# Four conditional layers on one core: the reaction term in a PSUM bank, the identity added behind the transposition, beta on GpSimd, a new order of the slots

## Chip, cores, metric

One Trainium2 chip, one core. The metric is device time in microseconds (us). An item is one of the 128 entries of the batch, a slot is one turn of the loops that take one item further on each engine. A transfer's landing time runs from its issue to the arrival of its completion.

## What is computed

x is 128 items of 128x512 (rows s by columns d), fp32. The reference, cut to what matters:

```python
def cond_residual(x, kind, lang, zX, zY, zR, cat, ...):
    a = tanh(x @ W1 + b1) @ v                       # one score per row
    p = softmax(where(mask[kind], a, -1e30))        # 128x128 per item
    x = x + (p @ x) / count(mask)                   # layer 0
    h = relu(x @ W1l[lang] + b1l[lang])
    y = x + h @ W2l[lang] + b2[lang]
    x = x + layernorm(y) * gamma[lang] + beta[lang] # layer 1
    lap_x, lap_y = second differences, reflected at the ends
    x = x + zX*lap_x + zY*lap_y + zR*x*(1-x)        # layer 2
    return x + x @ W3[cat] + b3[cat]                # layer 3, W3: 64 of 512x512
```

## The kernel before, in words

All five queues are written out by hand in raw form with semaphores: each engine has its own function `slot(s)`, which `run_slots` repeats, and every item is at a different stage on each engine (the number after `s -` says which item a call takes). Nothing else sets the order.

**Stages of an item.** PE projects the item's transpose (`attn_project`, `adapter_project`), ACT takes the tanh, PE spreads the scores and adds the mask (`attn_scores`), DVE finds the row maximum, ACT takes the exponentials, DVE makes the scale and writes scaled probabilities plus the identity (`mix_rows`, L713), PE transposes that (`mix_transpose`) and ACT moves the result (`move_mixT`). With the identity in it one matmul (`pool`, L402) gives x + pooled. DVE reads that bank twice: plus b2 (`add_b2`) and plus beta (`add_beta`, L777). PE adds the adapter (`adapter_up`, L411), DVE and ACT take mean and variance, GpSimd (POOL) the inverse root (`inverse_std`, L865), and `normalize` (L746) writes x2, the input of layer 2.

**Layer 2.** SP issues six DMAs per item (`shift_rows`, L281) that copy x2 from SBUF to SBUF one row up (`below`) and one row down (`above`); POOL adds the two (`sum_rows`, L885) and the left and right neighbours (`sum_columns`, L873). ACT writes c0 - zR*x2 into the SBUF buffer `react` (`reaction`, L539), POOL multiplies it by x2 (`react_times_x2`, L879), DVE adds the columns (`add_columns`, L754) and the rows (`add_rows`, L764) and so has x3.

**Layer 3.** PE transposes x3 (L419), ACT moves it, and `category` (L429) takes four 128x512 matmuls with the 1 MB matrix of the category into one of two banks `ps_out`. POOL adds x3 to the bias b3 (`add_b3`, L892), DVE adds bank and bias (`result`, L739), and SP stores.

**Loads.** Items are sorted by category, and a category's matrix is loaded once (`load_w3`, L259, skipped unless `fresh`) into one of two 1 MB halves. 55 of the 128 items bring a new matrix. In the sorted order (1 is a new one) they are
10011000110011100100001100011010 10001111110010100100001000010000 11000101000101001101110001010100 11010010110011011010001100101000.
b3 is read for every item and spread over 128 partitions (`load_b3`, L267, 256 KB written). SP's slot is: six shifts of item s, w3 of s, store of s-2, b3 of s; its registers for category, fresh and half are read (`load_params`) ahead of the wait for x2. xT and x are loaded from ACT's queue.

**Where items stand before.** x2 of item i is written at the end of DVE's slot i+1, x3 of i in slot i+3, the first category matmul of i is in PE's slot i+4 right behind the scores, and `result` of i in DVE's slot i+4. PE's slot begins with `pool`.

## Time and profile before

| | us |
|---|---|
| median of 3 runs | 1095.55 (1087.53 to 1095.93) |
| profiled execution | 1097.21 |
| its span, first to last instruction | 1095.4 |
| PE busy | 1055.9 (96%) |
| DVE busy | 956.5 (87%) |
| POOL busy | 710.9 (65%) |
| ACT busy | 504.8 (46%) |
| mean granted TensorE clock | 0.998 of full |

The profiled execution stands 1.8 us above its own span and 1.7 us above the median of the runs. Matmul ends are modelled and overlap the next start, so PE's real time for a piece is read from starts, or from the chain, which counts each stretch once. A DMA instruction's length is that of its issue, not of its transfer.

### The profile page before, as it was taken

What the parts mean: (1) busy time and instruction counts of PE and PEld (TensorE: products, weight loads), DVE (VectorE), ACT (ScalarE), POOL (GpSimd) and SP (SyncE); (2) the same over time, 40 slices, a digit from 0 to 9 for tenths busy, and PEclk for the clock granted to TensorE, in tenths of its full rate; (3) what the DMA queues carried; (4) which work ended last, traced back from release to release, by engine and by line L of the source; (5) the groups of instructions that cost most, each with busy time, mean ns of one, the idle gap of its engine ahead of it and who ended that gap; (6) DMA issues with size and microseconds to landing.
All of it is one profiled execution on the core that took longest, in us unless ns stands there. A gap on an engine that the chain in (4) does not pass through costs nothing.

```text
span 1095.4 us, 23744 instructions
## 1 busy us (share of the span) xinstructions
PE 1055.9 (96%) x4912; PEld 656.8 (60%) x4912; DVE 956.5 (87%) x1962; ACT 504.8 (46%) x1422; POOL 710.9 (65%) x665
## 2 busy tenths in 40 slices
PE   6799999999999999999999999999999999999996
PEld 3565666656655656666665566665666565566562
DVE  5799989989989899999888888989898898999994
ACT  3444444444444444445444444444444444444441
POOL 3467667666666676667657666767665766667765
PEclk9999999999999999999999999999999999999999
DMA  8688798678779977876786868887879788897873
GB/s 346 199 260 236 247 293 244 203 250 254 245 230 288 298 239 237 246 229 203 228 266 193 265 198 255 269 266 235 269 241 262 228 268 237 288 276 226 244 241 115
DMA packets 134732, 268.92 MB, mean 246 GB/s; under 512 B 29139, under 2 KB 29157, under 8 KB 127173
## 3 DMA queue, kind: packets, MB, share of 16 engines
q1 hardware_dynamic: 97476, 199.83, 58.7%
q10 hardware_dynamic: 37120, 67.58, 20.4%
q8 instruction: 49, 0.80, 0.3%
q14 instruction: 87, 0.70, 0.2%
HBM read 243.21 MB, written 33.55 MB: 253 GB/s over the span
## 4 chain that ended last, share of the span: by engine, by line
PE 54%; issue 21%; POOL 17%; DVE 6%; DVEq 1%; ACTq 0%; ACT 0%; DMA 0%; POOLq 0%; SPq 0%
PE ps_out L429 23%; POOL b_wide L892 6%; PE ps_adapt L411 6%; PE bank_hidden L383 6%; PE ps_attn L361 6%; PE ps_pool L402 6%; POOL neighbours L873 4%; POOL react L879 3%; PE ps_x3T L419 3%; POOL rstd L865 2%; DVE x L764 2%; PE bank_scores L372 2%; PE bank_hidden L395 1%; DVE res L739 1%; POOL above L885 1%
## 5 line engine op out<-in xcount | busy, mean ns | idle before, releaser
L429 PE MATMUL ps_out<-w3s,x3T 128*128 x1024 | 490.1, 601 | 2.3 <-ACT x3T L496 2.3
L885 POOL TENSOR_TENSOR above<-above,below 128x512 f32<-128x512 f32 x128 | 166.7, 1303 | 226.7 <-DMA above<-x 223.7
L429 PEld LDWEIGHTS ps_out<-w3s,x3T 128*128 128x128 f32 x1024 | 185.1, 191 | 190.6 <-issue 188.7
L764 DVE SCALAR_TENSOR_TENSOR x<-above,wide_rows,react 128x512 f32<-128x512 f32 x128 | 189.5, 1481 | 13.9 <-POOL above L885 12.5
L879 POOL TENSOR_TENSOR react<-react,x 128x512 f32<-128x512 f32 x128 | 175.5, 1371 | 2.4 <-ACT react L539 2.4
L892 POOL TENSOR_TENSOR b_wide<-b_wide,x 128x512 f32<-128x512 f32 x128 | 173.1, 1352 | 1.7 <-DMA b_wide<-in_b 1.7
L865 POOL TENSOR_TENSOR rstd<-var_eps,minus_half 128x1 f32<-128x1 f32 x128 | 70.2, 549 | 132.0 <-DVE var_eps L731 131.9
L517 ACT ACTIVATE square_junk<-ps_adapt,neg_mean 128x512 f32<-128x512 f32 x128 | 88.1, 688 | 139.1 <-DVE neg_mean L692 139.1
L411 PE MATMUL ps_adapt<-w_all,hid 128*128 x256 | 133.0, 601 | 12.6 <-DVE x L746 12.2
L383 PEld LDWEIGHTS bank_hidden<-w_all,xts 128*128 128x128 f32 x1024 | 124.4, 192 | 28.4 <-issue 26.4
L383 PE MATMUL bank_hidden<-w_all,xts 128*128 x1024 | 137.2, 277 | 0.0
L873 POOL TENSOR_TENSOR neighbours<-x 128x510 f32<-128x510 f32 x128 | 133.4, 1042 | 3.6 <-DVE x L746 3.6
L361 PE MATMUL ps_attn<-xts,w_attn 128*128 128x128 f32 x1024 | 135.3, 275 | 0.3 <-issue 0.3
L402 PE MATMUL ps_pool<-xs,mixT 128*128 128x512 f32 x256 | 131.0, 594 | 0.0
L361 PEld LDWEIGHTS ps_attn<-xts,w_attn 128*128 128x128 f32 x1024 | 124.6, 192 | 0.5 <-issue 0.5
L739 DVE TENSOR_TENSOR res<-ps_out,b_wide 128x512 f32<-128x512 f32 x128 | 87.2, 682 | 36.1 <-POOL b_wide L892 26.0
L713 DVE SCALAR_TENSOR_TENSOR mix<-probs,scale,ident 128x128 f32<-128x128 f32 x128 | 108.7, 849 | 0.3 <-issue 0.3
L686 DVE SCALAR_TENSOR_TENSOR ps_adapt<-ps_adapt,x_b 128x512 f32<-128x512 f32 x128 | 89.4, 698 | 17.0 <-PE ps_adapt L411 16.1
L539 ACT ACTIVATE react<-x,c_t,nzr_t 128x512 f32<-128x512 f32 x128 | 102.8, 803 | 2.8 <-DVE x L746 2.8
L502 ACT ACTIVATE probs<-bank_scores,neg_max 128x128 f32<-128x128 f32 x128 | 47.1, 368 | 118.3 <-DVE neg_max L679 118.0
L754 DVE SCALAR_TENSOR_TENSOR react<-neighbours,wide_rows,react 128x512 f32<-128x512 f32 x128 | 96.8, 756 | 0.5 <-POOL react L879 0.5
L722 DVE SCALAR_TENSOR_TENSOR ps_adapt<-ps_adapt,neg_mean,gamma_wide 128x512 f32<-128x512 f32 x128 | 95.5, 746 | 0.1
(111 smaller groups left out, 1281.3 us busy)
## 6 DMA issues: line engine op xcount, KB each, us to landing
w3s<-in_w SPq DMA_DIRECT2D x128, 1024.0 KB
xts<-in_xT ACTq DMA_DIRECT2D x128, 256.0 KB, 4.7
xs<-in_x ACTq DMA_DIRECT2D x128, 256.0 KB, 5.0
b_wide<-in_b SPq DMA_DIRECT2D x128, 256.0 KB, 4.2
out_x<-res SPq DMA_DIRECT2D x128, 256.0 KB, 3.4
below<-x SPq DMA_DIRECT2D x128, 252.0 KB
above<-x SPq DMA_DIRECT2D x128, 252.0 KB
below<-x SPq DMA_DIRECT2D x256, 2.0 KB
```

The source lines that it names most:

```text
L361: mm = pe.matmul(ps_attn, w1_attn[:, k * A:(k + 1) * A], xts[:, r, k, :], start=(k == 0), stop=(k == K - 1))
L383: mm = pe.matmul(ps_xw, xts[:, s.ring(2), k, :], w1_all[:, bass.ds(lang * (K * A) + k * A, A)], start=(k == 0), stop=(k == K - 1))
L402: pe.matmul(ps_pool[:, :], mixT[:, d.ring(2), :], xs[:, d.ring(2), :], start=True, stop=True).then_inc(pool_mm, 1)
L411: pe.matmul(ps_adapt[:, :], hid[:, g.ring(2), :], w2_all[:, bass.ds(lang * D, D)], start=True, stop=True).then_inc(adapt_mm, 1)
L429: mm = pe.matmul(ps_out[j.ring(2)][:, :], x3T[:, j.ring(2), k * P:(k + 1) * P], w3s[:, bass.ds(wslot * (K * D) + k * D, D)], start=(k == 0 ...
L539: nc.scalar.activation(react[:, h.ring(2), :], x2[:, h.ring(2), :], ACT.Identity, bias=c0_t[:, bass.ds(h.n, 1)], scale=nzr_t[:, bass.ds(h. ...
L713: nc.vector.scalar_tensor_tensor(mix[:, p, :], probs[:, p, :], scale[:, p:p + 1], ident[:, :], ALU.mult, ALU.add).then_inc(mix_ready, 1)
L764: nc.vector.scalar_tensor_tensor(x3[:, q, :], above[:, q, :], zy_t[:, bass.ds(i.n, 1)], react[:, q, :], ALU.mult, ALU.add).then_inc(x3_rea ...
L873: nc.gpsimd.tensor_tensor(neighbours[:, q, 1:D - 1], x2[:, q, 0:D - 2], x2[:, q, 2:D], ALU.add).then_inc(neighbours_ready, 1)
L879: nc.gpsimd.tensor_tensor(react[:, q, :], react[:, q, :], x2[:, q, :], ALU.mult).then_inc(react_x2_ready, 1)
L885: nc.gpsimd.tensor_tensor(above[:, q, :], above[:, q, :], below[:, q, :], ALU.add).then_inc(rows_ready, 1)
L892: nc.gpsimd.tensor_tensor(b3_wide[:, q, :], b3_wide[:, q, :], x3[:, q, :], ALU.add).then_inc(x3_b3_ready, 1)
```

## The change

- `react` becomes a single PSUM bank `ps_react`; the two banks `ps_out` become one. The product with x2 moves from POOL to DVE.
- ACT scales the probabilities (`scale_rows`), PE transposes them, and DVE adds the identity as it moves them out of PSUM (`add_identity`). `mix_rows` and `move_mixT` go.
- beta is no longer added by DVE from the bank: POOL adds a table of beta - b2 to `x1_b2` (`add_beta`); the table comes from one more small load and one subtraction at the start. `normalize` waits for it, and the bank of `pool` is free after `add_b2`.
- Every engine's slot is written in a new order. PE's begins with `attn_project`, does the last category matmul of item s-5, and the first three of item s-4 near its end. SP issues the shifts of s, then reads its registers, then w3 and b3 of item s-1, then the store of s-3. POOL's is beta and root of s, `add_b3` of s-2, columns and rows of s-1.

Core of the diff (the context rows of the slots are kept, their removed rows stand in the kernel above):

```diff
@@
...
-        ps_out = [pb("ps_out0"), pb("ps_out1")]
+        ps_react = pb("ps_react")
+        ps_out = pb("ps_out")
...
-        ps_wide = ps_out[0]
-        b2_banks = [ps_out[1], bank_scores]
+        ps_wide = ps_out
+        b2_banks = [ps_react, bank_scores]
...
@@
             def slot(s):
                 if s.inside(B):
-                    cat, fresh, wslot = load_params(sp, CAT, 3, s)
                     shift_rows(s)
-                    load_w3(s, cat, fresh, wslot)
-                if (s - 2).inside(B):
-                    item_m2, = load_params(sp, ITEM, 1, s - 2)
-                    store(s - 2, item_m2)
-                if s.inside(B):
-                    load_b3(s, cat)
-            run_slots(slot, 0, B + 1)
+                if (s - 1).inside(B):
+                    cat, fresh, wslot = load_params(sp, CAT, 3, s - 1)
+                    load_w3(s - 1, cat, fresh, wslot)
+                    load_b3(s - 1, cat)
+                if (s - 3).inside(B):
+                    item_m3, = load_params(sp, ITEM, 1, s - 3)
+                    store(s - 3, item_m3)
+            run_slots(slot, 0, B + 4)
             for r in range(2):
                 sp.wait_ge(res_out[r], 16 * (B // 2))
                 sp.wait_ge(w3_in[r], 16 * (B // 2))
@@
...
-            pe.wait_ge(pick_made, 1)
-            pe.wait_ge(row_rest, 2)
-            spread_b2(0)
-            spread_b2(1)
             def sort_param(what):
...
@@
-            spread_b2(2)
-            spread_b2(3)
+            pe.wait_ge(pick_made, 1)
+            pe.wait_ge(row_rest, 3)
+            for i in range(4):
+                spread_b2(i)
...
@@
-                    if j.is_at_least(2):
-                        pe.wait_ge(res_ready, j.upto(2))
+                    if j.is_at_least(1):
+                        pe.wait_ge(res_ready, j.upto(1))
...
-                    mm = pe.matmul(ps_out[j.ring(2)][:, :], x3T[:, j.ring(2), k * P:(k + 1) * P],
+                    mm = pe.matmul(ps_out[:, :], x3T[:, j.ring(2), k * P:(k + 1) * P],
...
             def slot(s):
...
+                if s.inside(B):
+                    attn_project(s)
+                if (s - 5).inside(B):
+                    wslot, = load_params(pe, WSLOT, 1, s - 5)
+                    category(s - 5, wslot, range(3, K))
+                if (s - 1).inside(B):
+                    adapter_hidden(s - 1)
+                    pool(s - 1)
                 if s.inside(B):
                     kind, = load_params(pe, KIND, 1, s)
...
+                    attn_scores(s, kind)
+                if (s - 4).inside(B):
+                    x3_transpose(s - 4)
                 if s.inside(B):
...
+                    lang, = load_params(pe, LANG, 1, s)
+                    adapter_project(s, lang)
+                if (s - 1).inside(B):
+                    lang_m1, = load_params(pe, LANG, 1, s - 1)
+                    adapter_up(s - 1, lang_m1)
+                if (s - 4).inside(B):
+                    wslot_next, = load_params(pe, WSLOT, 1, s - 4)
+                    category(s - 4, wslot_next, range(0, 3))
                 if s.inside(B):
                     mix_transpose(s)
...
+            run_slots(slot, 0, B + 4)
         @block.scalar
@@
...
+            act.dma_start(base_rows[:, :], lbase).then_inc(lrows_in, 16)
...
-            act.wait_ge(lrows_in, 16)
+            act.wait_ge(row_rest, 1)
...
-            act.wait_ge(row_rest, 1)
+            act.wait_ge(row_rest, 2)
...
@@
-            def move_mixT(b):
-                act.wait_ge(mixT_mm, b.upto())
+            def scale_rows(b):
+                p = b.ring(2)
+                act.wait_ge(scale_ready, b.upto())
+                act.wait_ge(probs_ready, b.upto())
...
-                    act.wait_ge(pool_mm, b.upto(2))
-                nc.scalar.activation(mixT[:, b.ring(2), :], ps_mixT, ACT.Copy).then_inc(mixT_ready, 1)
+                    act.wait_ge(mixT_mm, b.upto(2))
+                nc.scalar.activation(mix[:, p, :], probs[:, p, :], ACT.Copy, scale=scale[:, p:p + 1]
+                                     ).then_inc(mix_ready, 1)
...
             def relu(f, lang):
...
@@
-                if h.is_at_least(2):
-                    act.wait_ge(x3_ready, h.upto(2))
-                nc.scalar.activation(react[:, h.ring(2), :], x2[:, h.ring(2), :], ACT.Identity,
+                if h.is_at_least(1):
+                    act.wait_ge(x3_ready, h.upto(1))
+                nc.scalar.activation(ps_react[:, :], x2[:, h.ring(2), :], ACT.Identity,
...
@@
                 act.dma_start(xs[:, r], x[bass.ds(item, 1)].rearrange("o s d -> s (o d)")).then_inc(x_in[r], 16)
             def slot(s):
...
                 if s.inside(B):
                     item, = load_params(act, ITEM, 1, s)
+                    load_xT(s, item)
+                if s.is_first:
                     load_x(s, item)
...
                     for i in range(4, L):
                         move_b2(i)
+                if (s - 1).inside(B):
+                    attn_tanh(s - 1)
+                if (s - 2).inside(B):
+                    lang_m2, = load_params(act, LANG, 1, s - 2)
+                    relu(s - 2, lang_m2)
+                if (s - 4).inside(B):
+                    reaction(s - 4)
+                if (s - 5).inside(B):
+                    move_x3T(s - 5)
+                if (s - 1).inside(B):
+                    exponentials(s - 1)
+                    move_xw(s - 1)
+                if s.inside(B) and not s.is_first:
+                    load_x(s, item)
+                if (s - 4).inside(B):
+                    column_ends(s - 4)
+                if (s - 1).inside(B):
+                    scale_rows(s - 1)
                 if (s - 2).inside(B):
                     variance(s - 2)
...
+            run_slots(slot, 0, B + 4)
         @block.vector
@@
...
-            def mix_rows(b):
-                p = b.ring(2)
-                dve.wait_ge(scale_ready, b.upto())
+            def add_identity(b):
+                dve.wait_ge(mixT_mm, b.upto())
...
-                    dve.wait_ge(mixT_mm, b.upto(2))
-                nc.vector.scalar_tensor_tensor(mix[:, p, :], probs[:, p, :], scale[:, p:p + 1], ident[:, :],
-                                               ALU.mult, ALU.add).then_inc(mix_ready, 1)
+                    dve.wait_ge(pool_mm, b.upto(2))
+                nc.vector.tensor_tensor(mixT[:, b.ring(2), :], ps_mixT, ident[:, :], ALU.add).then_inc(mixT_ready, 1)
...
             def center(h, lang):
...
@@
-                nc.vector.tensor_tensor(res[:, o.ring(2), :], ps_out[o.ring(2)][:, :], b3_wide[:, o.ring(2), :], ALU.add
+                nc.vector.tensor_tensor(res[:, o.ring(2), :], ps_out[:, :], b3_wide[:, o.ring(2), :], ALU.add
...
             def normalize(h):
...
+                dve.wait_ge(x1_beta_ready, h.upto())
...
+            def react_times_x2(i):
+                q = i.ring(2)
+                dve.wait_ge(react_ready, i.upto())
+                nc.vector.tensor_tensor(ps_react[:, :], ps_react[:, :], x2[:, q, :], ALU.mult).then_inc(react_x2_ready, 1)
...
             def add_columns(i):
...
-                nc.vector.scalar_tensor_tensor(react[:, q, :], neighbours[:, q, :], zx_t[:, bass.ds(i.n, 1)],
-                                               react[:, q, :], ALU.mult, ALU.add).then_inc(columns_ready, 1)
+                nc.vector.scalar_tensor_tensor(ps_react[:, :], neighbours[:, q, :], zx_t[:, bass.ds(i.n, 1)],
+                                               ps_react[:, :], ALU.mult, ALU.add).then_inc(columns_ready, 1)
...
             def add_rows(i):
...
             def slot(s):
-                h = s - 1
-                if h.inside(B):
-                    lang, = load_params(dve, LANG, 1, h)
+                if (s - 1).inside(B):
+                    lang, = load_params(dve, LANG, 1, s - 1)
...
-                if h.inside(B):
-                    add_b2(h, lang)
-                    add_beta(h, lang)
                 if s.inside(B):
                     denominator(s)
...
+                    row_scale(s)
+                if (s - 1).inside(B):
+                    add_adapted(s - 1)
+                    mean(s - 1)
+                if (s - 3).inside(B):
+                    add_columns(s - 3)
                 if s.inside(B):
...
+                    add_identity(s)
                 if (s - 3).inside(B):
                     add_rows(s - 3)
+                if (s - 1).inside(B):
+                    add_epsilon(s - 1)
+                    center(s - 1, lang)
                 if (s - 4).inside(B):
                     result(s - 4)
...
+                if (s - 1).inside(B):
+                    normalize(s - 1)
+            run_slots(slot, 0, B + 4)
         @block.gpsimd
@@
...
+            pool.wait_ge(lrows_in, 2 * 16)
+            nc.gpsimd.tensor_tensor(lang_rows[:, :], lang_rows[:, :], base_rows[:, :], ALU.subtract).then_inc(row_rest, 1)
...
@@
+            def add_beta(h, lang):
+                q = h.ring(2)
+                pool.wait_ge(x1_b2_ready, h.upto())
+                if h.is_first:
+                    pool.wait_ge(beta_moved, L)
+                if h.is_at_least(2):
+                    pool.wait_ge(x2_ready, h.upto(2))
+                nc.gpsimd.tensor_tensor(x1_beta[:, q, :], x1_b2[:, q, :], beta_less_b2[:, bass.ds(lang * D, D)], ALU.add
+                                        ).then_inc(x1_beta_ready, 1)
             def inverse_std(h):
...
@@
                                         ).then_inc(x3_b3_ready, 1)
             def slot(s):
+                if s.inside(B):
+                    lang, = load_params(pool, LANG, 1, s)
+                    add_beta(s, lang)
+                    inverse_std(s)
                 if (s - 2).inside(B):
-                    sum_rows(s - 2)
+                    add_b3(s - 2)
                 if (s - 1).inside(B):
                     sum_columns(s - 1)
-                if (s - 3).inside(B):
-                    add_b3(s - 3)
-                if (s - 1).inside(B):
-                    react_times_x2(s - 1)
-                if s.inside(B):
-                    inverse_std(s)
-            run_slots(slot, 0, B + 2)
+                    sum_rows(s - 1)
+            run_slots(slot, 0, B + 4)
```

SP's queue from its first shifts on (`below`, `above` are the shifts, `w3s` the matrix, `b_wide` the b3 buffer), before:

```order
L281 DMA below<-x 126x512
L281 DMA above<-x 126x512
L281 DMA below<-x 1x16x32 x2
L281 DMA above<-x 1x16x32 x2
L259 ISA
L259 REGISTER_ALU
L259 DMA w3s<-in_w 128x2048
L267 ISA
L267 DMA b_wide<-in_b 128x512
L235 TENSOR_LOAD all_params
L281 DMA below<-x 126x512
```

After, behind the four rows of item 0's shifts, which read like the first four here (these are item 1's):

```order
L284 DMA below<-x 126x512
L284 DMA above<-x 126x512
L284 DMA below<-x 1x16x32 x2
L284 DMA above<-x 1x16x32 x2
L236 TENSOR_LOAD all_params
L260 ISA
L260 REGISTER_ALU
L260 DMA w3s<-in_w 128x2048
L268 ISA
L268 DMA b_wide<-in_b 128x512
```

The loads of item 0 have moved behind the shifts of item 1, and the register reads between those shifts and the loads. POOL's queue, one slot in the steady part, with what each instruction waits for, before:

```order
L885 TENSOR_TENSOR above<-above,below 128x512 [waits shift_in1]
L873 TENSOR_TENSOR neighbours<-x 128x510 [waits columns_ready,x2_ready]
L892 TENSOR_TENSOR b_wide<-b_wide,x 128x512 [waits b3_in0,x3_ready]
L879 TENSOR_TENSOR react<-react,x 128x512 [waits react_ready]
L865 TENSOR_TENSOR rstd<-var_eps,minus_half 128x1 [waits x2_ready,vareps_ready]
```

And after:

```order
L236 TENSOR_LOAD all_params
L860 ISA [waits x2_ready,x1_b2_ready]
L860 TENSOR_TENSOR x_beta<-x_b,beta_less_b 128x512
L868 TENSOR_TENSOR rstd<-var_eps,minus_half 128x1 [waits x2_ready,vareps_ready]
L889 TENSOR_TENSOR b_wide<-b_wide,x 128x512 [waits b3_in0,x3_ready]
L876 TENSOR_TENSOR neighbours<-x 128x510 [waits columns_ready,x2_ready]
L882 TENSOR_TENSOR above<-above,below 128x512 [waits shift_in1]
```

The addition of b3 (`b_wide`) now stands ahead of both neighbour sums and of the next slot's beta and root, where it stood behind the sums.

## Rows read from the trace of the kernel before

**Rows 1.** Chain that ended last, PE's slot around 500 us: start, us, what.

```profile
499.54 0.86 PE ps_pool L402 x2
...
502.45 2.58 PE ps_out L429 x6
505.02 0.11 PE bank_scores L389
...
506.03 0.89 PE ps_attn L361 x8
...
507.58 0.86 PE ps_pool L402 x2
```

**Rows 2.** Waits: who waited for whom, us in total, times, longest.

```profile
POOL above L885 <- DMA above<-x: 223.7, 113, 5.2
...
PE ps_adapt L411 <- DVE x L746: 12.2, 17, 1.3
...
PE bank_scores L389 <- DVE mix L713: 7.9, 4, 2.2
```

**Rows 3.** The page, costliest groups: busy us, mean ns, idle before.

```profile
L764 DVE SCALAR_TENSOR_TENSOR x<-above,wide_rows,react 128x512 f32<-128x512 f32 x128 | 189.5, 1481 | 13.9 <-POOL above L885 12.5
...
L865 POOL TENSOR_TENSOR rstd<-var_eps,minus_half 128x1 f32<-128x1 f32 x128 | 70.2, 549 | 132.0 <-DVE var_eps L731 131.9
...
L713 DVE SCALAR_TENSOR_TENSOR mix<-probs,scale,ident 128x128 f32<-128x128 f32 x128 | 108.7, 849 | 0.3 <-issue 0.3
```

**Rows 4.** Timeline of DVE around 500 us: start, us, instruction.

```profile
499.70 0.74 DVE L746 SCALAR_TENSOR_TENSOR x<-ps_adapt,rstd,x_beta 128x512 f32<-128x512 f32 x1
...
504.43 0.74 DVE L764 SCALAR_TENSOR_TENSOR x<-above,wide_rows,react 128x512 f32<-128x512 f32 x1
505.09 0.68 DVE L739 TENSOR_TENSOR res<-ps_out,b_wide 128x512 f32<-128x512 f32 x1
```

**Rows 5.** Timeline of SP's queue, the slot behind that x2 (items 57 and 58).

```profile
500.50 0.89 SPq L281 DMA_DIRECT2D below<-x  x1
...
503.68 1.74 SPq L281 DMA_DIRECT2D above<-x  x2
505.82 0.10 SPq L259 DMA_DIRECT2D w3s<-in_w  x1
506.60 0.37 SPq L272 DMA_DIRECT2D out_x<-res  x1
507.16 0.34 SPq L267 DMA_DIRECT2D b_wide<-in_b  x1
508.54 0.88 SPq L281 DMA_DIRECT2D below<-x  x1
...
511.53 1.22 SPq L281 DMA_DIRECT2D above<-x  x2
```

**Rows 6.** Timeline of POOL, 508 to 512 us.

```profile
508.14 1.27 POOL L885 TENSOR_TENSOR above<-above,below 128x512 f32<-128x512 f32 x1 [1.68 <-DMA above<-x]
509.37 1.04 POOL L873 TENSOR_TENSOR neighbours<-x 128x510 f32<-128x510 f32 x1
510.36 1.27 POOL L892 TENSOR_TENSOR b_wide<-b_wide,x 128x512 f32<-128x512 f32 x1
```

**Rows 7.** Line L267, all 128 b3 loads.

```profile
DMA to landing us min/median/max: 3.2/4.2/9.9
```

**Rows 8.** DMA issues from 445 to 470 us, no new matrix: count, KB, median landing.

```profile
b_wide<-in_b SPq DMA_DIRECT2D x3, 256.0 KB, 3.7
```

**Rows 9.** The same from 330 to 372 us, every matrix new.

```profile
b_wide<-in_b SPq DMA_DIRECT2D x5, 256.0 KB, 6.4
```

**Rows 10.** Timeline of DVE: first and last of 128 x2, and the last x3.

```profile
32.36 0.75 DVE L746 SCALAR_TENSOR_TENSOR x<-ps_adapt,rstd,x_beta 128x512 f32<-128x512 f32 x1
...
1074.01 0.75 DVE L746 SCALAR_TENSOR_TENSOR x<-ps_adapt,rstd,x_beta 128x512 f32<-128x512 f32 x1
...
1083.40 1.68 DVE L764 SCALAR_TENSOR_TENSOR x<-above,wide_rows,react 128x512 f32<-128x512 f32 x1 [2.72 <-POOL above L885]
```

109 lines of the change are left out of this document (21 added, 88 removed).

## The prediction

> **What bounds the kernel now.** I read the chain that ended last first, because PE is 96% busy. Its slot there has no hole: from one start of the pooling matmul to the next is 507.58 - 499.54 = 8.04 us [rows 1]. 127 such steps are 1021 us. From the end of the first x2 (33.1) to that of the last (1074.8) are 1041.7 us [rows 10], so PE loses 20.6 us in the steady part. The waits name them: 12.2 us for x2 ahead of the adapter matmul and 7.9 us for the mix ahead of its transposition [rows 2], together 20.1. The reader should see that PE bounds the kernel, that DVE is late now and then, and that no more than 21 us can be won in the loop. The matmuls are the same after the change.
>
> Next, why DVE is late. `add_rows` takes 1.48 us on average and the mix 0.85 [rows 3], but `add_rows` has a slot where it takes 0.74 [rows 4]. Both read two SBUF operands. The Trainium skill (SBUF — State Buffer, "SBUF: two separate sides") says that such a DVE instruction and a GpSimd one that reads SBUF shut each other out for the whole instruction. The averages here, twice the undisturbed length, agree.
>
> Last, the transfers, in SP's timeline and the landing times. Before, w3 and b3 of item i are issued right behind x2 of i and used three slots later, so their landing costs nothing. POOL does wait 223.7 us for the shifts [rows 2], without harm.
>
> **The change part by part.**
>
> *DVE's and POOL's work.* DVE loses the beta addition and the two instructions with two SBUF operands; it gains the product in PSUM (bounded by the PSUM and SBUF addition of 0.68 [rows 4] and the 0.74 of a three-operand one) and the identity, 128 wide (0.2 to 0.4; the 0.85 average holds the shut-outs). That is even in plain work and frees (1.48 - 0.74) x 128 = 95 us at `add_rows`, more at the mix. This is worth at most the 20.6 us above, and nothing if something else sets the slot. POOL swaps a product for a beta addition of the same form, 1.27 us. ACT swaps a 128-wide copy for a 128-wide scaling: nothing. The single `ps_out` is read by `result` while PE does some 3.5 us of other pieces, so I cost it at nothing; if that cover went, it would cost what `result` is late, 0.7 us a slot.
>
> *SP's queue.* Here is a wait the old order did not have. Loads of item i-1 are issued behind the shifts of item i, hence behind x2 of i. POOL's `add_b3` of i-1, which needs that b3, stands ahead of both sums of item i and ahead of beta and root of item i+2. DVE's `normalize` of i+2 stands behind `add_rows` of i. So x2 of i leads to b3 of i-1, to POOL's row, to x2 of i+2: a loop over two slots, whose length does not depend on where PE stands. Its parts:
>
> - x2 to the first shift 0.06 (500.44 to 500.50). Issuing the shifts 4.9 us (500.50 to 505.42) or 4.2 (508.54 to 512.75) [rows 5]; I take 4.5.
> - Reading three registers, now behind the shifts: between b3's issue ending (507.50) and the next shift (508.54) lie 1.04 us, part of it perhaps x2 [rows 5]; I take 0.95. Address of w3 0.4 (505.42 to 505.82), its issue 0.1, b3's 0.2. b3 is issued 6.2 us after x2.
> - Landing of b3. Over all slots 3.2 to 9.9 [rows 7]. Issue by issue, the 73 behind a repeated matrix have a median of 3.6, the 55 behind a new one 5.8, as the stretch without new matrices (3.7) and the one with only new ones (6.4) show [rows 8, 9]. The 1 MB goes ahead of it in the same queue.
> - POOL: `add_b3`, columns, rows. From the row sum's start to the next but one are 510.36 - 508.14 = 2.2 us, and the b3 addition takes 1.3 [rows 6]: 3.5.
> - DVE from there: `add_rows` 0.66 (504.43 to 505.09), epsilon 0.1, `center` as long, `result` 0.68, `normalize` 0.74 [rows 4]: 2.8. On POOL meanwhile a register read, beta 1.27 and the root 0.55 [rows 3], then `normalize`: 2.9 at most. I take 2.9.
>
> Sum with a repeated matrix: 6.2 + 3.6 + 3.5 + 2.9 = 16.2 us for two slots, against 2 x 8.04 = 16.08 of PE. It just binds. With a new matrix the 1 MB is issued 6.0 after x2 and b3 0.3 later. Before, b3 went 1.34 behind w3 and landed 5.8 later, with a 256 KB store between them; now there is no store between, so w3's issue to b3's landing is 7.1 less the store's part, which I put at 0.9: 6.2 to 6.4. That makes 12.3 + 6.4 = 18.7; I take 18.8.
>
> Both ends: 15.7 (shifts 4.2, landing 3.4) to 17.0 with a repeated matrix (POOL's path late, landing 4.2), and 17.4 (shifts 4.2, a landing near the shortest of the new ones) to 20 (landing like that of the stretch of new matrices, 6.4, and more).
>
> *The sum.* Let T(i) be the end of x2 of item i. T(i+2) is the later of T(i) + 16.2 (18.8 where the matrix of i-1 is new) and T(i+1) + 8.04. Walked along the order of new matrices given above, with T(0) = 0 and T(1) = 8.04: T(2) = 16.2, T(3) = 26.8 (item 0 is new), T(4) = 34.9, T(5) = 43.0, T(6) = 53.7, and so on to T(127) = 1129.7 (8.90 a slot). An average of the two lengths would give 8.66; the excess is that a late item drags its neighbour's chain with it.
>
> *Start and end.* Before, the first x2 is done at 33.1 and the last instruction ends 20.6 after the last x2. The start gains a subtraction on POOL (about 1.2 us as a row-wide one, beside the sorting) and moves the b2 rows behind the sorting: +1.0, between 0 and 3. At the end x3 of the last item came 10.3 us behind its x2 (1085.1 - 1074.8) [rows 10]; now it comes 6.2 + 3.6 + 3.5 + 0.8 = 14.1 behind: +3.8.
>
> Total against the profiled execution: 1.8 outside the span + 33.1 + 1.0 + 1129.7 + 20.6 + 3.8 = 1190 us. The profiled execution (1097.2) stands 1.7 above the median of the runs; I leave that in the rounding: 1188.
>
> The 1 MB itself has less time too. It is issued 6.0 after x2 of i and PE's first category matmul of i-1 comes some 10 after it when PE runs without holes. If it lands late, PE's three matmuls 2.58 and the transposition 0.11 [rows 1] follow, then `attn_project` 0.89 and the last 0.86 beside DVE's rows, and `result` and `normalize`, 1.4: with a landing of 5.7 that is 6.0 + 5.7 + 2.7 + 1.9 + 1.4 = 17.7, shorter than the 18.8 by b3, so it is not added.
>
> [...]
>
> **Rivals.**
>
> *PE stays without holes (faster).* DVE's shut-outs go, the 20.6 us come back and the loads land in time. For it: 16.2 is near 16.08, DVE's 95 us are real. Against: 55 slots with 1 MB ahead of b3. It decides where b3 behind a new matrix lands within 3.6 us of issue; the shortest of 55 is 3.8. Time: 1097.2 - 20.6 + 4.8 = 1081. The skill's rule on two SBUF operands gives this by itself.
>
> *The loop binds only a little (no change).* New matrices cost 16.5 for two slots: the same walk gives T(127) = 1037, 1098 in all. It needs landings some 2 us shorter than the trace's.
>
> *The 1 MB binds and not b3 (slower, less).* If b3 overtakes the matrix, new slots cost 17.4 and others 16.08: T(127) = 1072.6, 1133 us.
>
> *Transfers in a crowd (slower, more).* In the stretch of new matrices b3 takes 6.4 at the median [rows 9] with three slots of room; with less room xT, too, may be late. 17.0 and 20: T(127) = 1193, 1254 us.
>
> **Chances.** Forecast 0.58, PE without holes 0.06, no change 0.06, the 1 MB binds 0.17, crowd 0.13. The predicted time is the forecast's, 1188. The range leaves out the first two and the far end of the crowd: 1122 to 1248. About 1% is what a measurement tells here: faster 0.06, same 0.05, slower 0.89.
>
> **What would show it.** Right: POOL waits for b3 ahead of `add_b3` in most slots, 1 us or more in the mean and longest behind new matrices; PE's holes stand ahead of the adapter matmul (for x2), its busy share falls to some 89%; x2 of i to x2 of i+2 is near 16.2 or 18.8; `add_rows` takes 0.74 everywhere. Wrong: POOL's `add_b3` never waits for a DMA (then the loop does not exist), or PE's holes stand ahead of the category matmuls, released by the w3 DMA (then the 1 MB binds), or holes in front of `attn_project` released by xT.

## The result, and the profile after

| | before | after |
|---|---|---|
| median of the runs, us | 1095.74 (4 runs) | 1218.46 (4 runs, 1217.53 to 1223.32) |
| ratio | 1 | 1.1137, 95% interval 1.1063 to 1.1211 |
| profiled execution, its span | 1097.21, 1095.4 | 1223.32, 1221.5 |
| mean granted TensorE clock | 0.998 | 0.973 |

The change costs 11%. The page of the kernel after: busy times, granted clock, the chain that ended last by engine and by line, and four of the costliest groups.

```profile
PE 1099.6 (90%) x4912; PEld 663.6 (54%) x4912; DVE 818.8 (67%) x1962; ACT 518.1 (42%) x1422; POOL 681.1 (56%) x666
...
PEclk8899999999999999999999999999999999999998
...
PE 36%; SPq 21%; DMA 18%; POOL 12%; issue 7%; DVE 3%; DVEq 1%; ACT 1%; POOLq 0%; ACTq 0%
PE ps_out L428 16%; DMA b_wide<-in_b 15%; SPq L284 15%; SPq L236 4%; PE ps_adapt L410 4%; PE ps_attn L361 4%; PE bank_hidden L383 4%; POOL above L882 4%; PE ps_pool L401 3%; POOL x_beta L860 3%; POOL neighbours L876 3%; POOL b_wide L889 2%; DVE x L738 2%; SPq L260 2%; DMA w3s<-in_w 2%
...
L428 PE MATMUL ps_out<-w3s,x3T 128*128 x1024 | 508.0, 621 | 79.3 <-issue 63.9
L889 POOL TENSOR_TENSOR b_wide<-b_wide,x 128x512 f32<-128x512 f32 x128 | 162.4, 1269 | 466.9 <-DMA b_wide<-in_b 466.0
...
L751 DVE SCALAR_TENSOR_TENSOR ps_react<-neighbours,wide_rows,ps_react 128x512 f32<-128x512 f32 x128 | 96.7, 755 | 282.3 <-POOL neighbours L876 280.7
...
L761 DVE SCALAR_TENSOR_TENSOR x<-above,wide_rows,ps_react 128x512 f32<-128x512 f32 x128 | 95.3, 745 | 25.7 <-issue 22.1
```

The chain of before was PE's from slot to slot [rows 1]. Now only 36% of it is PE's; SP's queue (the shifts L284, the register reads L236), the landing of b3 and POOL's row hold half of it: the loop that the prediction describes. POOL waits 466 us for b3 ahead of `add_b3`, and DVE waits 281 us for the column sum that stands behind it. `add_rows` takes 745 ns instead of 1481 [rows 3], so DVE is freed, by 137.7 us of busy time, and none of it reaches the end.

DVE's timeline, the counterpart of [rows 10]: the first and the last x2, and the last x3.

```profile
44.01 0.75 DVE L738 SCALAR_TENSOR_TENSOR x<-ps_adapt,rstd,x_beta 128x512 f32<-128x512 f32 x1
...
1195.10 0.74 DVE L738 SCALAR_TENSOR_TENSOR x<-ps_adapt,rstd,x_beta 128x512 f32<-128x512 f32 x1
1209.23 0.75 DVE L761 SCALAR_TENSOR_TENSOR x<-above,wide_rows,ps_react 128x512 f32<-128x512 f32 x1 [0.47 <-POOL above L882]
```

From the first x2 (44.76) to the last (1195.84) are 1151.1 us, 9.06 a slot instead of 8.20. Before they were 1041.7; the first x2 comes 11.7 later, and from the last x2 to the end are 5.0 more.

Two turns of the loop. With a repeated matrix, from the timelines of SP, POOL and DVE, beginning at x2 of item 74 (ended 709.71):

```profile
709.74 0.88 SPq L284 DMA_DIRECT2D below<-x  x1
...
712.74 1.22 SPq L284 DMA_DIRECT2D above<-x  x2
715.50 0.11 SPq L260 DMA_DIRECT2D w3s<-in_w  x1
715.82 0.36 SPq L268 DMA_DIRECT2D b_wide<-in_b  x1
...
719.35 1.27 POOL L889 TENSOR_TENSOR b_wide<-b_wide,x 128x512 f32<-128x512 f32 x1 [3.11 <-DMA b_wide<-in_b]
...
721.57 1.27 POOL L882 TENSOR_TENSOR above<-above,below 128x512 f32<-128x512 f32 x1
722.93 0.75 DVE L761 SCALAR_TENSOR_TENSOR x<-above,wide_rows,ps_react 128x512 f32<-128x512 f32 x1
...
724.96 0.74 DVE L738 SCALAR_TENSOR_TENSOR x<-ps_adapt,rstd,x_beta 128x512 f32<-128x512 f32 x1
```

x2 of item 76 ends at 725.70, 15.99 behind: PE's own two slots. With a new matrix, here as the chain that ended last gives it (start, us, what), from x2 of item 78 (ended 745.46):

```profile
744.80 0.67 DVE x L738
...
745.48 0.88 SPq L284
...
749.76 1.16 SPq L236
...
751.31 0.36 SPq L260
...
751.89 6.07 DMA b_wide<-in_b
...
758.10 0.39 POOL b_wide L889
...
759.31 1.04 POOL neighbours L876
760.35 1.23 POOL above L882
761.58 1.23 POOL x_beta L860
...
763.73 0.67 DVE x L738
```

The register reads take 1.16 us behind the shifts, b3 lands 6.07 after its issue behind the 1 MB, and x2 of item 80 ends at 764.39, 18.93 behind. PE in the same stretch:

```profile
753.86 1.02 PE L410 MATMUL ps_adapt<-w_all,hid 128*128 x2
756.47 2.84 PE L428 MATMUL ps_out<-w3s,x3T 128*128 x6 [1.58 <-issue]
```

PE's largest hole stands ahead of the category matmuls and not of the adapter's. The page calls most of such idle time "issue". Sorted by item, the holes in front of the first category matmul sum to 76.2 us in 42 of the 55 items with a new matrix, and to 3.0 us in the 73 others; so nearly all of it is waits for w3. Two transfers are late, and the experiments had to tell them apart.

Medians below are over items 4 to 123, read from the timelines: two slots (x2 of n to x2 of n+2), apart by whether the matrix of n-1 is repeated or new. In the kernel after they are 16.6 and 19.3 us. Which items are new is read from the length of SP's w3 issue, 0.36 us for a load and 0.11 for a skipped one.

### The profile page after: what moved, and what is told of

It reads as the page before. It is cut to its first block, busy times and chain, and to the rows that moved or that the text cites. A ratio compares the mean times of both kernels' runs of the same rounds, so it can differ in the third digit from the quotient of the medians.

```text
span 1221.5 us, 24130 instructions
## 1 busy us (share of the span) xinstructions
PE 1099.6 (90%) x4912; PEld 663.6 (54%) x4912; DVE 818.8 (67%) x1962; ACT 518.1 (42%) x1422; POOL 681.1 (56%) x666
## 4 chain that ended last, share of the span: by engine, by line
PE 36%; SPq 21%; DMA 18%; POOL 12%; issue 7%; DVE 3%; DVEq 1%; ACT 1%; POOLq 0%; ACTq 0%
PE ps_out L428 16%; DMA b_wide<-in_b 15%; SPq L284 15%; SPq L236 4%; PE ps_adapt L410 4%; PE ps_attn L361 4%; PE bank_hidden L383 4%; POOL above L882 4%; PE ps_pool L401 3%; POOL x_beta L860 3%; POOL neighbours L876 3%; POOL b_wide L889 2%; DVE x L738 2%; SPq L260 2%; DMA w3s<-in_w 2%
## 5 line engine op out<-in xcount | busy, mean ns | idle before, releaser
L428 PE MATMUL ps_out<-w3s,x3T 128*128 x1024 | 508.0, 621 | 79.3 <-issue 63.9
L889 POOL TENSOR_TENSOR b_wide<-b_wide,x 128x512 f32<-128x512 f32 x128 | 162.4, 1269 | 466.9 <-DMA b_wide<-in_b 466.0
L751 DVE SCALAR_TENSOR_TENSOR ps_react<-neighbours,wide_rows,ps_react 128x512 f32<-128x512 f32 x128 | 96.7, 755 | 282.3 <-POOL neighbours L876 280.7
L545 ACT ACTIVATE attn<-ps_attn,vals 128x128 f32<-128x128 f32 x128 | 47.1, 368 | 318.2 <-PE ps_attn L361 316.7
L860 POOL TENSOR_TENSOR x_beta<-x_b,beta_less_b 128x512 f32<-128x512 f32 x128 | 163.2, 1275 | 13.3 <-DVE x_b L770 13.3
L761 DVE SCALAR_TENSOR_TENSOR x<-above,wide_rows,ps_react 128x512 f32<-128x512 f32 x128 | 95.3, 745 | 25.7 <-issue 22.1
L535 ACT ACTIVATE ps_react<-x,c_t,nzr_t 128x512 f32<-128x512 f32 x128 | 99.5, 777 | 10.4 <-DVE x L761 10.3
L489 ACT ACTIVATE x3T<-ps_x3T 128x512 f32<-128x512 f32 x128 | 76.5, 598 | 59.9 <-PE ps_x3T L418 59.9
L526 ACT ACTIVATE hid<-bank_hidden,vals 128x128 f32<-128x128 f32 x128 | 47.1, 368 | 119.4 <-PE bank_hidden L394 119.2
L738 DVE SCALAR_TENSOR_TENSOR x<-ps_adapt,rstd,x_beta 128x512 f32<-128x512 f32 x128 | 94.9, 741 | 0.2
```

Of the source, the lines that this page charges most:

```text
L428: mm = pe.matmul(ps_out[:, :], x3T[:, j.ring(2), k * P:(k + 1) * P], w3s[:, bass.ds(wslot * (K * D) + k * D, D)], start=(k == 0), stop=(k ...
L535: nc.scalar.activation(ps_react[:, :], x2[:, h.ring(2), :], ACT.Identity, bias=c0_t[:, bass.ds(h.n, 1)], scale=nzr_t[:, bass.ds(h.n, 1)]). ...
L738: nc.vector.scalar_tensor_tensor(x2[:, q, :], normed[:, :], rstd[:, q:q + 1], x1_beta[:, q, :], ALU.mult, ALU.add).then_inc(x2_ready, 1)
L860: nc.gpsimd.tensor_tensor(x1_beta[:, q, :], x1_b2[:, q, :], beta_less_b2[:, bass.ds(lang * D, D)], ALU.add).then_inc(x1_beta_ready, 1)
L889: nc.gpsimd.tensor_tensor(b3_wide[:, q, :], b3_wide[:, q, :], x3[:, q, :], ALU.add).then_inc(x3_b3_ready, 1)
```

## Experiments

All start from the kernel after. Theory A is the forecast's: the loop through b3 sets the time. Its main rival is the 1 MB.

**loads_early**: SP's order as before, all else as changed.

```diff
                 if s.inside(B):
+                    cat, fresh, wslot = load_params(sp, CAT, 3, s)
                     shift_rows(s)
-                if (s - 1).inside(B):
-                    cat, fresh, wslot = load_params(sp, CAT, 3, s - 1)
-                    load_w3(s - 1, cat, fresh, wslot)
-                    load_b3(s - 1, cat)
-                if (s - 3).inside(B):
...
-                    store(s - 3, item_m3)
+                    load_w3(s, cat, fresh, wslot)
+                if (s - 2).inside(B):
...
+                    store(s - 2, item_m2)
+                if s.inside(B):
+                    load_b3(s, cat)
```

> The changed kernel with SP's slot as it was before: w3 and b3 of item s behind the shifts of s, store of s-2. Theory A (the loop x2 -> b3 of the item before -> POOL -> x2 two items on sets the slot): the loop is gone, PE has no holes, x2 to x2 is 8.04 to 8.1 us, POOL waits for b3 in hardly any slot; 1223 - 1151 (the 127 steps of the changed kernel) + 1021 to 1030 = 1093 to 1102 us, minus 2 to 4 at the end. Rival B (the 1 MB that lands late at PE): the same time, since it too is early again. Rival C (the new order of the engines' own work, one ps_out bank, beta on POOL): the time stays above 1180 us.

Measured: 1092.14 us against 1093.58, ratio 0.999 (0.9966 to 1.0014). The page:

```profile
PE 1052.7 (97%) x4912; PEld 656.7 (61%) x4912; DVE 835.1 (77%) x1962; ACT 508.7 (47%) x1422; POOL 687.5 (63%) x666
```

and the wait of POOL for b3 (us in total, times, longest), as in the views of waits below:

```profile
POOL b_wide L889 <- DMA b_wide<-in_b: 144.8, 77, 5.4
```

The whole loss hangs on the order in SP's queue. The reader should also see that POOL still waits 144.8 us for b3 and nothing is lost by it: two slots take 16.0 and 16.2. A long wait says nothing until it lies on the chain.

**b3_early**: only b3 and the store go back to their old place; w3 stays behind the next item's shifts.

```diff
                 if s.inside(B):
+                    cat0, = load_params(sp, CAT, 1, s)
                     shift_rows(s)
...
                     load_w3(s - 1, cat, fresh, wslot)
-                    load_b3(s - 1, cat)
...
-                    store(s - 3, item_m3)
+                if (s - 2).inside(B):
...
+                    store(s - 2, item_m2)
+                if s.inside(B):
+                    load_b3(s, cat0)
```

> The changed kernel with b3 alone issued one item earlier; w3 stays behind the next item's shifts. Theory A: POOL's waits for b3 fall from 466 us to under 30; what is left is the 1 MB, two-slot steps of 17.4 to 17.7 us behind new matrices and 16.1 elsewhere: about 1135 to 1155 us. Rival B: b3 never mattered, the time stays within 1200 to 1223 us. Rival C: stays at 1218.

Measured: 1253.01 us, slower than the kernel after, where A had expected 1135 to 1155. The waits:

```profile
PE ps_out L430 <- DMA w3s<-in_w: 21.6, 12, 3.4
...
POOL b_wide L891 <- DMA b_wide<-in_b: 11.7, 3, 5.1
```

b3's wait is gone, as meant, but the store and b3 (two buffers) of the early order stand in SP's queue behind `result` of item s-2, which PE now brings late; so w3 of the next item is issued 7.3 us after x2 instead of 6.3, and two slots with a new matrix take 20.6. One late transfer was exchanged for another. The experiment moved two things and so doesn't say what b3 alone is worth.

**w3_early**: only w3 goes back ahead of the others, b3 of s-1 stays behind.

```diff
+                    cat0, fresh, wslot = load_params(sp, CAT, 3, s)
                     shift_rows(s)
+                    load_w3(s, cat0, fresh, wslot)
                 if (s - 1).inside(B):
-                    cat, fresh, wslot = load_params(sp, CAT, 3, s - 1)
-                    load_w3(s - 1, cat, fresh, wslot)
+                    cat, = load_params(sp, CAT, 1, s - 1)
                     load_b3(s - 1, cat)
```

> The changed kernel with w3 alone issued one item earlier (behind the shifts of its own item); b3 of the item before comes behind it. Theory A: b3 is as late as in the changed kernel, still behind 1 MB when the next matrix is new: 1190 to 1220 us, POOL's waits for b3 stay above 400 us, PE's waits for w3 (13.8 us) go to 0. Rival B: the 1 MB was the cause, so the time falls to about 1100 us.

Measured: 1272.08 us, where A had expected 1190 to 1220.

```profile
POOL b_wide L890 <- DMA b_wide<-in_b: 504.5, 121, 9.0
```

No wait for w3 is left among PE's, and the kernel is slower still: w3 of s waits for the half that item s-2 reads, b3 stands behind that wait, is issued 7.6 us after x2 in every slot and lands late behind repeated matrices too (19.0 and 19.5). In both misses the price lay in what stood in line behind the moved load.

**b3_behind_sums**: SP's queue as changed; POOL adds b3 behind both sums, so x3 no longer waits for b3.

```diff
-                if (s - 2).inside(B):
-                    add_b3(s - 2)
                 if (s - 1).inside(B):
                     sum_columns(s - 1)
                     sum_rows(s - 1)
+                if (s - 2).inside(B):
+                    add_b3(s - 2)
```

> The changed kernel, loads as late as there, but POOL adds b3 behind its two neighbour sums. Theory A: it is the place in POOL's order that hands b3's lateness to x2; add_b3 then holds up only the next beta and root (landed b3 at 12.7 behind x2 + 1.3 + 0.3 + 1.3 + 0.6 + 0.7 = 16.9 with a new matrix, 14.1 with a repeated one), the 1 MB takes over: 1135 to 1165 us. Rival B (the 1 MB alone): unchanged at 1218. If the sums waited for the shifts instead, POOL's wait would move to L882 and the time would lie between.

Measured: 1175.0 us, 10 above A's range; two slots 16.0 and 18.3.

```profile
POOL b_wide L889 <- DMA b_wide<-in_b: 258.8, 112, 5.4
```

POOL's wait for b3 is still 258.8 us, but it now ends behind the sums. PE's holes ahead of the category matmuls are nearly those of the kernel after (72.6 against 76.2 us at new matrices), though the kernel is 43 us faster.

**b3_three**: b3 in its early place with three buffers, so that neither its load nor the store holds SP up; POOL's order as changed.

```diff
-        b3_wide = sb("b3_wide", [P, 2, D])
+        b3_wide = sb("b3_wide", [P, 3, D])
...
                     load_w3(s - 1, cat, fresh, wslot)
-                    load_b3(s - 1, cat)
+                if s.inside(B):
+                    load_b3(s, cat0)
```

> The changed kernel with b3 one item earlier in a third buffer, so that SP does not wait for the result of the item two before (as it does in b3_early). Theory A plus SP blocked by that wait in b3_early: POOL's waits for b3 vanish, w3 is issued some 6.5 us behind x2 instead of 7.3, the two-slot steps are those of b3_behind_sums, 16.0 and 18.4 us: 1170 to 1190 us. If b3 early were bad by itself: near 1253.

Measured: 1175.96 us; two slots 16.0 and 18.2.

```profile
PE ps_out L430 <- DMA w3s<-in_w: 17.3, 13, 3.4
...
POOL b_wide L892 <- DMA b_wide<-in_b: 3.1, 1, 3.1
```

Two ways of taking b3 out of the loop, one by POOL's order and one by a buffer, end within 1 us of each other. b3 alone is worth 43 us (1218.5 - 1175); behind it stands the 1 MB, whose loop is 1 us shorter for two slots. The prediction had this second limit at 17.7, the runs have it at 18.2 to 18.3.

**two_matrices**: a matrix counts as new only in the first four places of the order, so two of the 55 are loaded and b3 keeps its late place. The other items are multiplied by one of these two: the kernel leaves out what they need and serves to measure time alone.

```diff
-            nc.vector.tensor_scalar(vals[:, FRESH:FRESH + 1], seen_col[:, :], 0.0, None, ALU.is_equal)
+            then(nc.vector.tensor_scalar(vals[:, FRESH:FRESH + 1], seen_col[:, :], 0.0, None, ALU.is_equal))
+            nc.vector.tensor_scalar(vals[:, FRESH:FRESH + 1], rank_col[:, :], 4.0, vals[:, FRESH:FRESH + 1],
+                                    ALU.is_lt, ALU.mult)
```

> The changed kernel, but only the first two matrices are ever loaded, one into each half; the others' items use those two. Theory A (b3's loop): every two-slot step is that of a repeated matrix, 16.6 us, still above 16.08, POOL waits for b3 in every slot: 127 x 8.29 = 1052, with start and end 1120 to 1130 us. Rival B (only the 1 MB matters): no holes, 8.04 us a slot, 1093 to 1097 us.

Measured: 1116.52 us, 3.5 below A's range; two slots 16.4 and 16.2, by the old places of the new matrices.

```profile
POOL b_wide L891 <- DMA b_wide<-in_b: 386.3, 126, 7.7
```

The late order without its 1 MB transfers costs 24 us against loads_early (1092.1); the other 102 of 126 need the 1 MB, as a transfer ahead of b3 or as w3 itself.

**b3_ahead**: b3 is issued ahead of w3.

```diff
-                    load_w3(s - 1, cat, fresh, wslot)
                     load_b3(s - 1, cat)
+                    load_w3(s - 1, cat, fresh, wslot)
```

> The changed kernel with b3 issued ahead of w3 in the same place of SP's queue. Theory A: b3 lands 3.7 us after issue for every item, POOL's waits for it fall to the level of repeated matrices (10.2 behind x2 in all slots); w3 is issued 0.4 later and has 256 KB ahead of it, so the slots of new matrices are now set by the 1 MB, 18.3 (b3_behind_sums) plus 0.4 to 1.2: 18.7 to 19.5 for two slots, 16.6 elsewhere; 1190 to 1220 us, little or nothing gained. Rival (b3 behind the 1 MB is the only cost): 1125 us as in two_matrices.

Measured: 1284.27 us, the slowest of all; two slots 16.0 and 21.2. The waits:

```profile
POOL b_wide L889 <- DMA b_wide<-in_b: 275.5, 94, 8.1
...
PE ps_out L428 <- issue: 115.8, 36, 5.4
```

b3, issued 0.9 us earlier, is in time: `add_b3` begins 9.9 us behind x2 at a new matrix instead of 12.9. But w3, issued only 0.2 later than in the kernel after, lands later: the last of its semaphore updates comes 6.5 us behind its issue instead of 5.2. Neither theory had that. Against the 18.3 of b3_behind_sums, two slots with a new matrix are 2.9 us longer: the issue of w3 comes 0.3 later, PE's first category matmul another 1.2 (6.8 instead of 5.6 behind the issue), and from there to x2 are 1.7 more (medians of the slots in which PE waits, which need not add up). Of that last part 1.5 are the first six category matmuls, 4.3 instead of 2.8 us, at TensorE's lower clock (section on the hardware below).

**regs_ahead**: the three register reads go ahead of the wait for x2.

```diff
             def slot(s):
+                if (s - 1).inside(B):
+                    cat, fresh, wslot = load_params(sp, CAT, 3, s - 1)
                 if s.inside(B):
                     shift_rows(s)
                 if (s - 1).inside(B):
-                    cat, fresh, wslot = load_params(sp, CAT, 3, s - 1)
                     load_w3(s - 1, cat, fresh, wslot)
```

> The changed kernel with SP's three register reads for the loads ahead of the shifts again, nothing else: the loop x2 -> b3 -> x2 is 0.9 us shorter and the way to w3 too. Theory A: x2 to w3's issue 5.4 us instead of 6.3; two-slot steps 18.4 (new) and 16.1 (repeated, now PE's own 2 x 8.04) instead of 19.3 and 16.6; by the walk 46 us less: 1165 to 1180 us. Rival (the lateness is made by DMA traffic, not by SP's chain of issues): less than 10 us gained.

Measured: 1194.05 us; two slots 16.0 and 19.0. w3 is issued 4.9 us after x2 instead of 6.3, b3 as much earlier, but behind a new matrix `add_b3` begins only 0.4 earlier (12.5 instead of 12.9). The repeated slots fall to PE's own 16.0; of the 1.4 us earlier issue the new ones keep a third, since b3's landing there got longer by 0.8 us (6.7 instead of 5.9), and that of the 1 MB by 1.1 (6.3 instead of 5.2). In the first 5 us of the 1 MB the queue of x and xT moved 262 KB instead of 10 (medians), as w3 now follows the load of xT by 1.0 us instead of 2.4; that this is the cause is not shown. 24 us were gained, half of what A gave.

**base_first** and **early_and_base**: the second table of rows (`lbase`) is loaded ahead of `w1a`; once in the kernel after, once together with loads_early.

```diff
-            act.dma_start(w1_attn[:, :], w1a).then_inc(w1a_in, 16)
             act.dma_start(lang_rows[:, :], lrows).then_inc(lrows_in, 16)
             act.dma_start(base_rows[:, :], lbase).then_inc(lrows_in, 16)
+            act.dma_start(w1_attn[:, :], w1a).then_inc(w1a_in, 16)
```

> The changed kernel with only the order of ACT's three first loads changed (both small tables first). First x2 at 34 us instead of 44.8, nothing else: 1208 us, between 1206 and 1212. If the start is not set by that table: 1218.

Measured: 1223.92 us, a miss. `base_rows` landed after 3.0 us instead of 11.2 and the first x2 ended at 39.95 instead of 44.76; the steady part of this one execution was 5.3 longer and took it back; why is open. So I tried it where the loop doesn't bind:

> The changed kernel with SP's loads as early as before and, on ACT's queue, the two small tables ahead of the attention weights. Both theories of the steady part: 8.04 us a slot as in loads_early, and the start shorter by what the table of beta minus b2 was late (first x2 41.3 us there, 33 to 35 here): 1092 - 7 = 1082 to 1086 us, so faster than the kernel before by 0.8 to 1.2%. If the table is just as late behind the large loads of the other queue: no change against loads_early.

Measured: 1089.02 us against 1096.12, ratio 0.9946 (0.992 to 0.9971): faster than before by half a per cent, less than the expected 0.8 to 1.2%, and with start_as_before the fastest here. The first x2 ended at 37.84; in loads_early, with the late table, at 41.32.

**start_as_before**: early_and_base, and two of the four b2 rows are spread ahead of the sorting again.

```diff
+            pe.wait_ge(pick_made, 1)
+            pe.wait_ge(row_rest, 3)
+            spread_b2(0)
+            spread_b2(1)
             def sort_param(what):
...
```

> early_and_base with the first two b2 rows spread ahead of the sorted parameters again, as in the kernel before. If that order is what keeps the start long: first x2 at 34 us instead of 37.8, 1089 - 4 = 1085 us, ratio to before 0.990. If the start is long because PE waits and its clock is low there, or because of the new slot order: 37 to 38 us and 1089.

Measured: 1088.59 us against 1093.79, ratio 0.9949 (0.9915 to 0.9983), the first x2 at 40.62. The place of the b2 rows isn't what makes the start long.

The chain of this execution runs through a load instead, the xT of item 1:

```profile
21.05 8.88 DMA xts<-in_xT
29.98 2.08 PE ps_attn L364 x8
```

and in the kernel before the same load:

```profile
15.00 1.33 ACTq L565
```

There ACT issued it ahead of moving the last b2 and beta rows, and it landed at 18.7 us. The new order of ACT's slots issues it behind them, and it landed at 29.9 here and at 29.4 in early_and_base. PE's slot now begins with `attn_project`, so the adapter of item 0 stands behind that landing. With the b2 rows early PE began item 0 at 20.8 us instead of 23.5 and had to wait longer for item 1. What an earlier issue would give was not run.

**react_sbuf**: early_and_base with the reaction term in an SBUF buffer, the part of the change that frees DVE.

```diff
+        react_sb = sb("react_sb", [P, D])
...
-                nc.vector.scalar_tensor_tensor(x3[:, q, :], above[:, q, :], zy_t[:, bass.ds(i.n, 1)],
-                                               ps_react[:, :], ALU.mult, ALU.add).then_inc(x3_ready, 1)
+                nc.vector.scalar_tensor_tensor(x3[:, q, :], above[:, q, :], zy_t[:, bass.ds(i.n, 1)],
+                                               react_sb[:, :], ALU.mult, ALU.add).then_inc(x3_ready, 1)
```

> early_and_base with the reaction term in one SBUF buffer instead of the PSUM bank; order, engines and loads unchanged. Theory D (DVE instructions with two SBUF operands wait for whole GpSimd instructions, and the PSUM bank is what took that away): add_rows rises from 0.74 us to over 1.0 in the mean, the product and add_columns rise too, single ones to 1.7 or more; x2 comes later than PE's slack of 1.2 us allows in part of the slots: 8.1 to 8.6 us a slot, 1095 to 1160 us. Rival E (the new order alone brought the 20 us of the steady part): DVE's means stay at 0.74 and the time at 1089.

Measured: 1094.53 us against 1094.43, ratio 1.0002 (0.9972 to 1.0031). Groups by line (busy us, mean ns, idle before), in early_and_base:

```profile
L751 DVE SCALAR_TENSOR_TENSOR ps_react<-neighbours,wide_rows,ps_react 128x512 f32<-128x512 f32 x128 | 96.7, 755 | 32.9 <-POOL neighbours L876 30.7 <-issue 2.0
L761 DVE SCALAR_TENSOR_TENSOR x<-above,wide_rows,ps_react 128x512 f32<-128x512 f32 x128 | 94.8, 740 | 21.2 <-POOL above L882 13.3 <-issue 7.8
```

and in react_sbuf:

```profile
L752 DVE SCALAR_TENSOR_TENSOR react_sb<-neighbours,wide_rows,react_sb 128x512 f32<-128x512 f32 x128 | 171.2, 1337 | 12.9 <-POOL neighbours L877 11.6 <-DVE react_sb L745 1.0 <-issue 0.3
L762 DVE SCALAR_TENSOR_TENSOR x<-above,wide_rows,react_sb 128x512 f32<-128x512 f32 x128 | 136.7, 1068 | 10.2 <-POOL above L883 9.7 <-issue 0.3
```

DVE is busy 963.8 instead of 835.8 us, and from the first x2 to the last are 1028.4 us instead of 1021.8. The bank saves DVE 128 us and the kernel 6.6 of the 20 us that its steady part lost before; the ratios to before, 0.9946 with the bank and 1.0002 without, say about the same. So neither theory holds alone: single `add_rows` take up to 1.69 us as D has it, but the rest of the change, the new order with it, brings the larger part of the 20 us without the bank.

## Why the prediction was right

The forecast's mechanism decided, on its side and in its range (1218.5, range 1122 to 1248); its time of 1188 is 30 us short. Against the profiled execution (1223.3 against 1190) the 33 us are: the first x2 10.7 later than forecast (44.8, not 34.1), the steady part 21.4 longer (1151.1, not 1129.7), the end 1.2 longer. The time alone can't tell the forecast from "transfers in a crowd" (1254), since it lies nearly midway; the landings do, 3.6 and 5.9 us instead of the crowd's 4.2 and 6.4. Most of its signs came too: POOL waited for b3 in 121 of 128 slots, PE was busy 90%, `add_rows` never took over 0.75 us.

- *"SP's queue: a wait the old order did not have"*: right. Putting SP's order back returns all of the loss (loads_early), taking b3 out of the loop returns 43 us (b3_behind_sums, b3_three).
- *"b3 is issued 6.2 us after x2"*: too small, measured 6.6, and 6.9 behind a new matrix (6.3 forecast). This is the mis-sized term. I took 0.95 for three register reads, from a gap between two transfers in which SP wasn't known to wait for x2, and 4.5 for the shifts; from the shifts' end to w3 are 1.56 us, where 1.35 were counted, and the shifts take 4.65 in the mean. The slips of 0.4 and 0.5 give two slots of 16.6 and 19.3 instead of 16.2 and 18.8. The same walk with these gives T(127) = 1157.6; measured are 1151.1. Two small slips leave the sum as it is: 6.0 + 3.5 + 2.9 are 12.4 and not 12.3 (18.8 was taken), and in the order of new matrices items 63 and 64 are the new ones and not 64 and 65, by SP's issues of w3; the walk ends at 1129.7 either way.
- *Landing 3.6, and 6.2 to 6.4 counted from w3's issue behind a new matrix*: nearly right. b3 lands 3.6 behind its issue, and 5.9 behind it where w3 went ahead (medians); from w3's issue that is 6.5. In the kernel before that load had 5.8 with a store between; the landing times read from a kernel in which they cost nothing held in one in which they cost all.
- *"POOL: 3.5"* and *"DVE from there 2.9"*: 3.49 and 2.82, right.
- *"The 1 MB is not added"*: right by its rule, since b3's loop is the longer one, and too easily put aside. It has 18.2 to 18.3 against b3's 19.3. I had 17.7, from 6.0 for the issue, 5.7 for the landing and 6.0 for the rest; in b3_behind_sums these are 6.2, 5.6 and 6.1 in the slots where PE waits for it (medians, which need not add up to 18.3). And it showed where I had said the opposite: "PE's holes ahead of the adapter matmul" was wrong, they stand ahead of the category matmuls, 76.2 us in all, which the prediction had listed as a sign against itself. That sign alone would have made me name the wrong transfer: with b3 out of the loop the same holes stay and 43 us go. PE's holes show the transfer that PE meets first, and the loop's length, by x2 to x2, shows the one that binds.
- *DVE freed, worth at most 20.6 us*: right. Of 1041.7 us the best order leaves 1021.8, which is PE's 127 slots at 8.04. The Trainium skill (SBUF — State Buffer, "SBUF: two separate sides") says that a DVE instruction with two SBUF operands and a GpSimd one that reads SBUF shut each other out for the whole instruction. The trace agrees in react_sbuf: `add_rows` 1068 ns instead of 740, the column addition 1337 instead of 755, and POOL's beta addition 1427 instead of 1273. That run doesn't reach before's 1481; how much of that difference is the order of the work is not shown.
- *"The start +1.0, between 0 and 3"*: wrong, it is 11.7. `base_rows` is a load that I left out of the sum: it landed 11.2 us after its issue. That accounts for some 3.5 to 5 (41.3 to 37.8 with the old order of SP, 44.8 to 40.0 with the new one). A further 5 to 7.5 remain (first x2 at 37.8 to 40.6 in the kernels that load it early, 33.1 before). The place of the b2 rows is excluded by start_as_before; the chains of early_and_base and start_as_before run through the xT of item 1, a second load that the sum left out, and no run tests what it is worth.
- *The end, "+3.8"*: 5.0. Its reasoning held: x3 of the last item comes 14.1 us behind its x2, as forecast. The rest stands behind it: the last eight category matmuls take 6.45 us, where before they took 5.39, since more of them fall into TensorE's lower clock (granted 0.56 of full between 1211.7 and 1218.0, and 0.68 between 1086.6 and 1091.9 before).
- *Rivals*: "the 1 MB binds and not b3" (1133) is what b3_behind_sums and b3_three build; they took 1175, since it lasts 18.3 and not 17.4. "Transfers in a crowd" didn't come, by the landings above.

## What to carry to other kernels

Where one queue issues in order, a load placed behind a transfer that waits for data inherits that wait; if the load's user stands ahead of the work that makes the next data, that is a loop, and its length is found by adding issue, landing and the users' row, whatever the busy shares say. Before a load is moved to a "better" place, list what stands behind it in the queue: b3_early (with its store) and w3_early each moved one load to an earlier place and lost 35 to 54 us by what they held up. Work taken off an engine that isn't the bound is worth only the holes that it makes in the one that is.

## What was not expected of the hardware

**A small load behind a large one on another queue.** DMA issues in the first 5 us of the kernel after, KB and us to landing:

```profile
lang_rows<-in_lrows ACTq DMA_DIRECT2D x1, 192.0 KB, 3.1
base_rows<-in_lbase ACTq DMA_DIRECT2D x1, 192.0 KB, 11.2
```

Two equal loads from one queue, 3.1 and 11.2 us; between them SP issues the 2,560 KB of `w_all`. Ahead of it, in base_first, the second takes 3.0, and `w1a`, now the last, takes 12.2 instead of 2.8.

**A large load behind a broadcast.** From issue to the last semaphore update the 1 MB took 5.2 us in the kernel after and 5.3 in b3_behind_sums, but 6.5 in b3_ahead, with the 256 KB of b3 in front of it (medians). It took 6.3 in regs_ahead too, without that, so b3 isn't the only thing that delays it. Why is open; no run separates packets from queue.

**TensorE's clock.** PE's timeline, in the kernel after at 61 us and in a later slot without a hole, six category matmuls each:

```profile
61.18 5.48 PE L428 MATMUL ps_out<-w3s,x3T 128*128 x6 [3.19 <-DMA w3s<-in_w]
...
711.72 2.74 PE L428 MATMUL ps_out<-w3s,x3T 128*128 x6
```

Behind the hole they take exactly twice as long, and the granted clock is 0.50 of full there: the lower of the two levels, 1.2 instead of 2.4 GHz. Of the 128 such groups 12 took over 3.2 us in the kernel after and 34 in b3_ahead. The windows of the slow group in the kernel after and of b3_ahead's steady part give (duration, PE busy, then the granted clock, DMA share and GB/s):

```profile
61.20:66.60 5.40, 5.40 (x7) 0.50 0.78 261
...
42.00:1260.00 1218.00, 1083.18 (x4771) 0.94 0.70 211
```

against, in the kernel after, these for a stretch of the start and for its steady part:

```profile
16.00:24.00 8.00, 4.75 (x15) 0.59 0.29 113
44.00:1196.00 1152.00, 1057.87 (x4772) 0.98 0.72 223
```

So a hole in PE costs more than its length: b3_ahead's steady part is 106 us longer than that of b3_behind_sums, 59 in holes and 47 in longer matmuls (PE busy 1083 against 1036 us). The slow groups stood behind holes of about 2 us or more (the last item's behind one of 4.4 ahead of its transposition), but a hole of 3.7 us in b3_ahead brought none; what else decides is open. With two levels a mean of 0.98 is 4% of the time at the lower one, and 0.94 is 12%, an estimate from these means. That is part of why b3_ahead and the two early misses (0.952 and 0.956) lie above their expectations.
